# Band attention of a two-layer network rebuilt on the structure of its full attention

## The reference

```python
idx = jnp.arange(1024)
mask = jnp.abs(idx[:, None] - idx[None, :]) <= 16        # a band of 33 keys
mask = mask.at[0, :].set(True).at[:, 0].set(True)       # token 0 sees and is seen by all
scores = jnp.einsum('bnsd,bntd->bnst', q, k) * 8 ** -0.5  # 16 heads of 8 numbers
scores = jnp.where(mask, scores, -inf)
attn = softmax(scores)
out = jnp.einsum('bnst,bntd->bnsd', attn, v) -> (2, 1024, 128)
return out @ Wo.T
```

## Time and profile before

| | us |
|---|---|
| median of 3 runs (1248.14 to 1253.72) | 1250.81 |
| the profiled execution, its own time | 1252.19 |
| its span, first to last instruction | 1250.5 |
| TensorE busy | 1065.1 (85%) |
| VectorE busy | 897.3 (72%) |
| ScalarE busy | 741.3 (59%) |
| GpSimd busy | 184.7 (15%) |

### The profile page before, as it was taken

How to read it: one execution, slowest core, us unless ns; L and a number is a source line. 1 busy time by engine, 2 the same in 40 slices (tenths; PEclk the granted TensorE clock), 3 DMA queues, 4 the chain that set the end, 5 groups by cost and what they waited for, 6 DMA issues and landing times.

```text
span 1250.5 us, 32345 instructions
## 1 busy us (share of the span) xinstructions
PE 1065.1 (85%) x12934; PEld 532.7 (43%) x12934; DVE 897.3 (72%) x1221; ACT 741.3 (59%) x1496; POOL 184.7 (15%) x341
## 2 busy tenths in 40 slices
PE   6457887888648799999999998877999999999986
PEld 3135676764214333333334444533333344444443
DVE  4554554556465479999999991364899999999635
ACT  2250222223822339989999994222599899999921
POOL 9500434330008000000000000000000000000000
PEclk9668878779977799999999998678999999999977
DMA  2140212100000523322010100007322300101000
GB/s 82 64 126 23 85 56 85 52 2 1 1 0 0 174 83 67 70 48 49 18 29 18 26 21 20 0 1 227 59 62 52 77 20 20 26 20 27 19 14 34
DMA packets 65913, 58.05 MB, mean 46 GB/s; under 512 B 24944, under 2 KB 50032, under 8 KB 65648
## 3 DMA queue, kind: packets, MB, share of 16 engines
q1 hardware_dynamic: 65776, 56.14, 17.1%
HBM read 29.08 MB, written 26.84 MB: 45 GB/s over the span
## 4 chain that ended last, share of the span: by engine, by line
DVE 39%; PE 27%; issue 17%; POOL 8%; DMA 4%; ACT 3%; SPq 2%; POOLq 0%; DVEq 0%; ACTq 0%
DVE nmf L1355 33%; PE wide L565 16%; PE bank L565 10%; POOL big L535 4%; DMA KQs<-m_dram 3%; ACT xcsq L931 2%; DVE xcsq L1138 1%; DVE nmt L1364 1%; DVE res L1138 1%; SPq L371 1%; ACT big L931 1%; POOL KQs L502 1%; DVE big L1439 1%; DVE x L1138 1%; DMA kq_dram<-big 1%
## 5 line engine op out<-in xcount | busy, mean ns | idle before, releaser
L1355 DVE TENSOR_REDUCE nmf<-wide 128x1 f32<-128x1024 f32 x512 | 586.9, 1201 | 34.7 <-PE wide L565 34.5
L931 ACT ACTIVATE big<-wide 128x512 f32<-128x512 f32 (+2 forms) x773 | 441.9, 601 | 149.3 <-PE wide L565 116.1
L565 PE MATMUL bank<-big,V 128*9 128x128 f32 x8192 | 319.2, 274 | 11.8
L565 PE MATMUL wide<-big,KQs 48*128 48x512 bf16 x1024 | 308.0, 381 | 4.3 <-DVE nmf L1355 3.2
L931 ACT ACTIVATE big<-bank 128x512 f32<-128x512 f32 (+3 forms) x489 | 237.5, 506 | 82.4 <-PE bank L689 61.5
L565 PEld LDWEIGHTS bank<-big,V 128*9 128x9 f32 x8192 | 176.7, 90 | 232.2 <-ACT big L931 222.0
L565 PE MATMUL wide<-KQs,big 50*128 50x512 bf16 x683 | 233.5, 381 | 8.0 <-DMA KQs<-m_dram 6.9
L565 PE MATMUL bank<-KQs,big 50*128 50x512 bf16 x341 | 130.0, 381 | 4.2 <-DMA KQs<-m_dram 3.2
L547 POOL CAST nms<-nmf 128x4 bf16<-128x4 f32 x128 | 23.8, 186 | 715.5 <-DVE nmf L1355 715.5
L1302 DVE TENSOR_REDUCE nm<-wide 95x11 f32<-95x1408 f32 x32 | 51.7, 1620 | 57.5 <-PE wide L565 57.4
L565 PEld LDWEIGHTS wide<-KQs,big 50*128 50x128 bf16 x683 | 52.4, 93 | 83.4 <-ACT big L931 56.0
(11 more groups left out here) (190 smaller groups left out, 1050.6 us busy)
## 6 DMA issues: line engine op xcount, KB each, us to landing
kq_dram<-big SPq DMA_DIRECT2D x48, 256.0 KB, 4.1
o_dram<-big SPq DMA_DIRECT2D x128, 64.0 KB, 1.6
KQs<-k_dram SPq DMA_DIRECT2D x48, 132.0 KB
big<-kq_dram SPq DMA_DIRECT2D x32, 192.0 KB, 4.1
KQs<-kq_dram SPq DMA_DIRECT2D x32, 192.0 KB, 4.6
KQs<-q_dram SPq DMA_DIRECT2D x16, 293.9 KB
m_dram<-nmt SPq DMA_DIRECT2D x128, 8.0 KB
KQs<-m_dram SPq DMA_DIRECT2D x128, 2.0 KB
```

The costliest lines, as they stand in the source:

```text
L565: return nc.tensor.matmul(o, l, r, start=start, stop=stop, **kw)
L931: return nc.scalar.activation(o, i, f, **kw)
L1355: nc.vector.tensor_reduce(nmf[:, (s0 + i) % 4, c:c + 1], wide[:, k:k + 2, :].rearrange("p g c -> p (g c)"), AX.X, ALU.max, negate=True).th ...
```

## The change

It rewrites the band attention after the full one:
- The projections go batch by batch, q, k, v (`chunks`). v is kept in fp32 alone. q and k parts are held for one batch at a time; SP stores each batch with 12 transfers and loads operands of 48 rows by groups of 4 heads, even heads in the lower, odd heads in the upper half of the rows. `xwin` and other scratch areas move.
- The maxima are split in two, not three, by GpSimd, turned by VectorE and sent through memory; they run 5 units ahead.
- Scores come in three banks (4, 4 and 3 windows). ScalarE takes three exponentials a unit and copies the values out (`weights`, `values_out`, at most two units of values in flight). The values are fp32 with 9 stationary columns. Output and denominators of a unit go through memory and are divided once per batch.
- TensorE issues 22 dense products at the entry and one after each group of the first five units (`keep_busy`, now from `maskk`).
- Query 0's chain is cut into `zero_scores`, `zero_turn`, `zero_values`, `zero_column` and placed between the first units.
- The ones rows are 2 more rows of the k arrays in memory, stored once at the start, for the full attentions too.

Whole functions that go are left out; "..." marks what is left out.

```diff
+AHEAD_W = 5
+WG = ((0, 4), (4, 4), (8, 3))
+OW = 3 * QT
...
+            for b in range(B):
+                for t, n in QCH:
+                    yield "q", b, xp[:, b, HALF + t * QT:HALF + (t + n) * QT], n * QT, t * QT
+                for t, n in WG:
+                    yield "k", b, xwin[:, b, t:t + n, :], n * P, t * P
+                for t, n in WG:
+                    yield "v", b, None, n * P, b * WT + t
...
+        LOADS_W = {2: 4, 6: 5, 10: 6, 14: 7}
...
+            sp.wait_ge(ones_rows, 1)
+            for dram in (kw_dram, kf_dram):
+                cols = dram.shape[2] * H * 2 // P
+                sp.dma_start(dram[KR:KR + 2, :, :].rearrange("r h c -> (r h c)").rearrange("(p c) -> p c", c=cols),
+                             onesb[:, 0:cols]).then_inc(ones_out, 16)
...
+                def store(b, k):
+                    sp.wait_ge(part3, 2 * len(WG) * b + len(WG) * (2 - k))
+                    for j, i in enumerate(ROW_PARTS[k]):
+                        if k:
+                            dst, src = qw_dram[j * D:j * D + D, :, QW * b:QW * b + QW], partq[:, i, :]
+                        else:
+                            dst, src = kw_dram[j * D:j * D + D, :, KW * b:KW * b + KW], partk[:, i, :]
+                        sp.dma_start(dst.rearrange("d h c -> h d c"), src).then_inc(partw_out[k], 16)
+                def load_group(g):
+                    b, p0 = g // 4, g % 4 * 2
+                    for odd in range(2):
+                        r, h = 64 * odd, slice(2 * p0 + odd, 2 * p0 + 4, 2)
+                        sp.dma_start(kopw[r:r + KR + 2, p0:p0 + 2, KW * b:KW * b + KW],
+                                     kw_dram[:, h, KW * b:KW * b + KW]).then_inc(opw_in[2 * g + odd], 16)
+                        sp.dma_start(qopw[r:r + KR, p0:p0 + 2, QW * b:QW * b + QW],
+                                     qw_dram[:, h, QW * b:QW * b + QW]).then_inc(opw_in[2 * g + odd], 16)
+                def shift(u):
+                    b, p, r, h = place_w(u)
+                    sp.wait_ge(nm_out[u % 4], 16 * (u // 4 + 1))
+                    rows = mw_dram[u, 0:2 * WT, 0:QT].rearrange("(a y) q -> a y q", a=2)
+                    sp.dma_start(qopw[r + KR:r + KR + 2, p, QW * b:QW * b + QW].rearrange("a (y q) -> a y q", q=QT),
+                                 rows).then_inc(nm_in[u % 8], 16)
+                def heads_out(u):
+                    b, p, r, h = place_w(u)
+                    sp.wait_ge(pv_evac, u + 1)
+                    sp.dma_start(ow_dram[b, h, :, :].rearrange("r (c q) -> c r q", c=4),
+                                 ow[:, u % 4, :]).then_inc(o_out[u % 4], 16)
+                def batch_in(b):
+                    for j in range(4):
+                        sp.wait_ge(o_out[j], 16 * H * (b + 1) // 4)
+                    sp.dma_start(denw[:, b, :], ow_dram[b, :, D, 0:S].rearrange("h (g q) -> h g q", g=8)).then_inc(w_den, 16)
+                    sp.dma_start(aT[:, S * b:S * b + S], ow_dram[b, :, 0:D, 0:S]).then_inc(w_in, 16)
+                for b in range(B):
+                    for k in (1, 0):
+                        store(b, k)
+                    if b == 0:
+                        sp.wait_ge(ones_out, 32)
+                        for k in range(2):
+                            sp.wait_ge(partw_out[k], 96)
+                        load_group(0)
+                        load_group(1)
+                for k in range(2):
+                    sp.wait_ge(partw_out[k], 96 * B)
+                sp.wait_ge(win_const, 1)
+                for u in range(AHEAD_W - 1):
+                    turned(u, mw_dram[u, :, :])
+                    if u:
+                        shift(u - 1)
+                    if u == 1:
+                        load_group(2)
+                load_group(3)
+                for u in range(UNITS):
+                    if u + AHEAD_W - 1 < UNITS:
+                        turned(u + AHEAD_W - 1, mw_dram[u + AHEAD_W - 1, :, :])
+                    if u + AHEAD_W - 2 < UNITS:
+                        shift(u + AHEAD_W - 2)
+                    if u in LOADS_W:
+                        load_group(LOADS_W[u])
+                    if u > 1:
+                        heads_out(u - 2)
+                        if u == H + 3:
+                            batch_in(0)
+                heads_out(UNITS - 2)
+                heads_out(UNITS - 1)
+                batch_in(1)
...
+            pool.memset(onesb[:, :], 1.0).then_inc(ones_rows, 1)
...
+            def keep_busy(count, o):
+                cols = maskk[:, :, :].rearrange("p t k -> p (t k)")[:, 0:512]
+                for _ in range(count):
+                    mm(o, identb[:, :], cols)
...
+                pe.wait_ge(part3, QK_W)
+                pe.wait_ge(part_v, CHUNKS_W - QK_W)
                 pe.wait_ge(win_const, 1)
+                pe.wait_ge(tw, 2)
+                keep_busy(2, bk(6))
+                keep_busy(20, bk(7))
...
+                def mask_maximum(u, g):
+                    n = len(WG) * u + g
+                    t, k = WG[g]
+                    if g == 0 and u % H % 4 < 2:
+                        pe.wait_ge(opw_in[2 * (4 * (u // H) + u % H // 4) + u % 2], 32)
+                    if n >= 3:
+                        pe.wait_ge(wx_read, n - 2)
+                    mm(bk(g)[0:QT, 0:k * P], identb[0:QT, 0:QT],
+                       maskq[0:QT, t:t + k, :].rearrange("p t k -> p (t k)"))
+                def maximum(u, g, y):
+                    b, p, r, h = place_w(u)
+                    t = WG[g][0]
+                    q0, k0 = QW * b + QT * y, KW * b + P * y
+                    ins = mm(bk(g)[0:QT, (y - t) * P:(y - t + 1) * P], qopw[r:r + KR, p, q0:q0 + QT],
+                             kopw[r:r + KR, p, k0:k0 + P], start=False, stop=True, skip_group_check=True)
+                    if y == t + WG[g][1] - 1:
+                        ins.then_inc(wx_ready, 1)
+                def mask_scores(u, g):
+                    n = len(WG) * u + g
+                    t, k = WG[g]
+                    if u == 0:
+                        pe.wait_ge(g0a, 2)
+                    if g == 0:
+                        pe.wait_ge(nm_in[u % 8], 16 * (u // 8 + 1))
+                    if n >= 3:
+                        pe.wait_ge(ws_exp, n - 2)
+                    mm(bk(3 + g)[:, 0:k * QT], identb[:, :], maskk[:, t:t + k, :].rearrange("p t k -> p (t k)"))
+                def scores(u, g, y):
+                    b, p, r, h = place_w(u)
+                    t = WG[g][0]
+                    q0, k0 = QW * b + QT * y, KW * b + P * y
+                    ins = mm(bk(3 + g)[:, (y - t) * QT:(y - t + 1) * QT], kopw[r:r + KR + 2, p, k0:k0 + P],
+                             qopw[r:r + KR + 2, p, q0:q0 + QT], start=False, stop=True, skip_group_check=True)
+                    if y == t + WG[g][1] - 1:
+                        ins.then_inc(ws_ready, 1)
+                def values(u):
+                    b, p, r, h = place_w(u)
+                    pe.wait_ge(ws_exp, len(WG) * (u + 1))
+                    if u == 0:
+                        pe.wait_ge(g0v, 4)
+                    if u == 1:
+                        pe.wait_ge(g0v, 15)
+                    if u >= 2:
+                        pe.wait_ge(pv_evac, u - 1)
+                    for j in range(3):
+                        for c in range(4):
+                            y = 3 * c + j
+                            if y < WT:
+                                ins = mm(bk(6 + u % 2)[32 * c:32 * c + D + 1, QT * j:QT * j + QT],
+                                         V[:, b * WT + y, h, :], ptw[:, u % 4, QT * y:QT * y + QT])
+                    ins.then_inc(wv_done, 1)
+                pe.wait_ge(q0_const, 1)
+                pe.wait_ge(g0v, 1)
+                for u in range(AHEAD_W):
+                    for g, (t, k) in enumerate(WG):
+                        mask_maximum(u, g)
                         for y in range(t, t + k):
+                            maximum(u, g, y)
+                        keep_busy(1, bk(7))
+                    if u == 0:
+                        zero_scores(0)
+                    if u == 2:
+                        zero_scores(1)
+                    if u == 3:
+                        zero_turn()
+                zero_values()
+                for u in range(UNITS):
+                    ahead = u + AHEAD_W < UNITS
+                    if u == 1:
+                        zero_column()
+                    for g, (t, k) in enumerate(WG):
+                        mask_scores(u, g)
+                        if ahead:
+                            mask_maximum(u + AHEAD_W, g)
                         for y in range(t, t + k):
+                            scores(u, g, y)
+                            if ahead:
+                                maximum(u + AHEAD_W, g, y)
+                        if g == 1 and u:
+                            values(u - 1)
+                values(UNITS - 1)
...
+                pe.wait_ge(wx_read, len(WG) * UNITS)
```

(69 more changed lines are left out.)

590 lines of the change are left out of this document (179 added, 411 removed).

## The result

The changed kernel takes 1242.8 us (median of 20 executions, 1223.6 to 1253.4) against 1251.5 us for the kernel before (20 executions, 1243.9 to 1258.9). The ratio is 0.989, 95% interval 0.986 to 0.992: faster by 1.1%, a small change but clear of noise, and outside the predicted range of 1168 to 1222 us. Ratios here are made from the undisturbed executions of both kernels, so that one can differ a little from the quotient of the medians.

A forecast was written before the change was run, and what follows sets the result against it. TensorE was taken as the band loop's bound, slowed by waits for k rows and the lower clock after them. 1250.5 - 19.4 (entry and prologue) - 43.4 (loop) + 4.5 (tail) = 1192.2 us; forecast 1192, range 1168 to 1222.

The forecast's parts named there:

- Entry: Band attention's start to first maxima: these at 74.8 us instead of 107.7, bounds 70 to 82.
- Prologue: First maxima to first scores: five units 12.5 us plus query 0's 14, together 26.5, so the loop starts at 101.3.
- Unit at full clock: TensorE's work for one band loop unit: 3.15 us, of it pairs 0.77, values 0.59, changes of shape 0.77.
- Output: Band attention's tail, last unit's output to memory and back: 17 us against 12.5, so +4.5.
- Loop: The band attention's 32 units: 104.6 us against 148.0, so -43.4.
- query 0's quotients ... 3 us: Loop stall term: ten dependent VectorE operations hold TensorE before unit 1, 3 us of 8 us of stalls.
- low clock: Rival: gaps of TensorE hold the band loop at 1.2 GHz, unit 4.76 us, loop 154, total 1242; chance 0.06.
- Late operands: Rival: the 19.9 us of waiting stays in another form behind heavier traffic, or the clock dips; 1212 us, chance 0.20.
- Wrong if: Refuting conditions: VectorE ends the loop's chain, a full-clock unit outside 2.6 to 3.9 us, or entry store waits beyond 62.
- the prediction's own bounds: Around 1192 us: array costs in the loop's units -15 and +22, entry and tail -9 and +11.
- The forecast's sign: Whole kernel faster, meaning under 1244.6 us: chance 0.93, same 0.03, slower 0.04.

The follow-up runs named there:

- experiment 1: Changed kernel with query 0's column product moved from ahead of unit 1 to the middle of unit 3: 1220.6 us.
- experiment 9: experiment 5 with SyncE loading each unit's shift rows one unit later: 1185.1 us, ratio 0.947 to the kernel before.
- experiment 11: experiment 9 with the two loads returning batch 0's heads and denominators moved from unit 19 to 30, reciprocal behind the loop: 1183.0 us, ratio 0.947.
- experiment 12: experiment 9 with query 0's column product put back ahead of unit 1, as in the changed kernel: 1244.1 us, ratio 0.991.
- experiment 6: Changed kernel with three dense products of 128 rows ahead of the value products in every unit from unit 2: 1211.8 us, ratio 0.965.
- experiment 8: experiment 6 with the three added products cut from 128 to 48 rows: 1283.7 us, ratio 1.024.
- experiment 2: Changed kernel with 16 dense products ahead of query 0's column product, left in its old place: 1224.7 us, ratio 0.978.
- experiment 3: Changed kernel with 20 dense products ahead of unit 5, the gap at query 0 left in: 1231.6 us, ratio 0.975.
- experiment 4: Changed kernel with query 0's whole chain run before the entry's dense products: 1256.2 us, ratio 1.002.
- experiment 5: experiment 1 with operand groups 3 to 7 loaded one transfer a unit: three executions at 1177 to 1184 us (ratio 0.943), four at 1207 to 1213.

## Why the prediction was wrong

By its own steps:

- **Entry: right in kind, 6 us too long.** First maxima at 69.1 us for 74.8. The stores went from 42.42 and the load at 57.32, inside the bound of 62. The dense products cost 4.9 us (22 x 0.21, all at full clock), not 7.6; the first projection stood at 35.1, not 39.3, since the copies of the windows on VectorE take 6.3 us now, for 12.2, which the prediction had not looked at. So 4.2 of the 5.7 us come from ahead of the entry.
- **Prologue: right.** 26.1 us for 26.5, with the clock at 0.50 for 3 us of it (from 87.7).
- **Unit at full clock: right.** 2.98 us in experiment 1 for 3.15. Pairs follow each other at 0.05 us, the lower bound, not 0.07; 22 values take 0.61 for 0.59; masks, by their columns, 1.02. What is left for the changes of shape is 2.98 - 0.55 - 0.61 - 1.02 = 0.80 us, for 0.77. The Trainium skill (TensorEngine Tiling (Array Packing), Key Properties) names a drain at each change; these rows agree, with some 0.11 us.
- **Output: right.** 15.5 us for 17.
- **Loop: wrong, and this is the step that failed.** The prediction wrote 27 x 3.15 + 5 x 2.3 + 8 = 104.6 us. It took 158.8 to the end of the last values, 54 us more; the other terms together came out 7.6 us less (5.7 + 0.4 + 1.5). 1192.2 + 54.2 - 7.6 = 1238.8, against the span of 1240.4. The units' counts and costs at full clock were right; the fault is the term "query 0's quotients ... 3 us". It priced the wait as time in which nothing runs, and left out what the wait does to all that follows: 5.12 us for 2.98, 27 times. Experiments 9, 11 and 12 show it: with the waits mended the loop is 99 and 94 us, shorter than forecast, and with the one stall put back it is 157.8.
- **The rival "low clock" was the right one, with 0.06.** It gave a unit of 4.76 for 5.12, a loop of 154 for 158.8, and 1242 us. That the total fits to 1 us is luck: its loop was 4.8 us too short, and the entry, prologue and output that it shared with the forecast were 7.6 too long. What spoke against it was that the full attention keeps 1.00. That row was the wrong one to weigh. The old band loop shows what a wait does to a band loop: after each of its six waits for k rows, 2.80 to 3.72 us, it ran low, and was back at full clock 7 to 13 us later (one case is in the earlier trace rows), with score and maximum products of 125 to 128 rows. The change makes those 48 to 50 rows high, and the clock does not come back. Experiments 6 and 8 show that rows matter for products added to this loop; that the loop's own lower rows are the cause is argued from them, not shown.
- **Height alone is not the rule.** The changed kernel's full attention has products of 48 and 50 rows too, in pairs, but 512 columns long. TensorE waits there nine times for 1.09 to 1.83 us, and the clock falls after one of them, 1.75 us. It is back 3.4 us later, with no product of the dense kind between (timeline and windows):

```profile
462.72 0.39 PE L556 MATMUL wide<-KQs,big 50*128 50x512 bf16 x1 [1.75 <-DMA KQs<-m_dram]
...
463.00:466.40 3.40, 3.40 (x42) 1.05 (x40) 2.21 (x3) 2.17 (x4) 0.00 (x0) 0.50 0.03 2
466.40:476.00 9.60, 9.40 (x168) 3.73 (x164) 9.31 (x11) 9.29 (x20) 0.77 (x4) 1.00 0.07 18
890.30:900.00 9.70, 9.41 (x164) 3.78 (x165) 8.99 (x10) 8.92 (x19) 0.39 (x2) 1.00 0.08 17
```

  The last row is after the wait of 1.83 us: the clock was kept. So "a wait, then low to the end" belongs to the band loop with its short products, its own weights for each and its changes of shape.
- **"Late operands", 0.20, was real, but hidden** by the slow loop; it appears as soon as the loop is fast (1 to 5).

None of the conditions under "Wrong if" came up: the unit at full clock, the entry and VectorE all stayed inside their bounds, since none of them looks at how long the loop runs at which clock. What did show it were the clock digits and the time of the last values, 253 us for 206. By the prediction's own bounds the upper end would be 1192 + 22 + 11 = 1225, not 1222; the result lies outside both.

The forecast's sign came out right, but not through the loop: first scores come 25.5 us earlier than before (95.2 for 120.7), the loop takes 10.8 us more (158.8 for 148.0) and the output 3.0 more. The costs of the single instructions were sound; it left out that a stall is also a change of state. What stays open: what in the band loop keeps the clock down, why it came back by itself once, in experiment 9, and why one execution of the changed kernel is as short as 1224 us. Its mean clock, 0.886, is the highest of the twenty, so the clock may have come back in part there too; only one execution of each kernel has a profile. Of the added products, 128 rows were compared with 48 and nothing between, and pairs of 48 rows were not tried.

## What to carry to other kernels

When a change puts packed, low and short products (here 48 to 50 rows, 95 to 128 columns) in a loop, price each stall in it not only by its length but by the rest of the loop at the lower clock, unless the trace shows that such a loop wins the clock back: here 3.4 us cost 55 to 59. Full-height products after the stall brought it back in experiments 3 and 6. Look in the trace of before at how the clock comes back after a wait, and ask whether the products that brought it back are still there. And a loop made faster must be checked against transfers that its slowness had hidden; small urgent stores belong ahead of, or between, large early loads.

## What the runs showed of the hardware

- TensorE busy in 45.00 of 45.00 us and in 152.5 of 153.0 stayed at a granted clock of 0.50 throughout, with 48 to 50 row products in pairs, masks and 9-column values between. Being busy did not bring it back. The Trainium skill (TensorE: Matmul & The Clock Gate, What's actually happening) ties the full clock to how busy the engine has been. The windows of this band loop do not bear that out, and the measurement decides; those of the full attention, which came back to 1.00 while it was busy, agree with it. The section HAM oscillation of that page of the Trainium skill tells of a kernel whose waits for transfers throw the clock back each time. The band loop's waits of 1.32 to 3.30 us for shift rows agree; the full attention's do not: eight of its nine waits of 1.09 to 1.83 us left the clock at 1.00, and so did one of 2.38 us in experiment 12 (ending at 890.13). The length of a wait alone does not tell whether the clock falls.
- The full clock, once held, was kept by the band loop for 95 us, through waits of up to 0.9 us (experiment 11), and in experiment 1 through one of 1.0.
- The clock can fall without a long wait: in the changed kernel's prologue it is 0.51 from 87.7 to 91.0 us, TensorE busy in 3.30 of 3.30 us, after a wait of 0.52 us (ending at 83.99) and 22 small transposes of 16 rows and 16 columns.
- Two half-height products with 95 and 128 columns, each with its own weights, start together and the next pair 0.05 us later.
- The load that waits for an 8 KB store could go 5.3 us after the store's issue when a transfer of 275 KB and one of 142.5 KB were issued just ahead of the store (experiment 5, 133.53 and 138.79), and 7.7 us after it behind four operand transfers of 0.94 MB in all and one of 142.5 KB (experiment 1, 118.56 and 126.23).
